# A decoder megakernel on Trainium2: the recurrence's epilogue joined to the routed layer

## The reference, cut to what matters

```
# fifth: a recurrence over 128 steps; of each step only this matters here
y = tanh(g @ L_gy_w.T + L_gy_b + s @ L_sy.T) @ L_yy_w.T + L_yy_b
x = layernorm(x + y)
# sixth: routed layer with sign weights
routing   = softmax(x @ gate_w.T)                    # 8 experts
in_scale  = routing @ in_channel_scale
out_scale = routing @ out_channel_scale
out = (x * in_scale) @ sign(weight).T * out_scale + bias
x = layernorm(x + out)
```

## Time and profile before

| | us |
|---|---|
| median of 3 runs | 3505.43 (3503.76 to 3507.91) |
| the profiled execution's own time | 3504.24 |
| its span in the trace | 3502.4 |

### The profile page before, as it was taken

The page is one execution under the profiler, slowest core; times in us unless marked ns, Lnnn a source line. Parts: engine busy times, 40 slices in busy tenths (PEclk is TensorE's granted clock), DMA queues, the critical chain, the costliest instruction groups (busy, mean ns, idle before and its releaser), DMA issues. The chain is left out here.

```text
span 3502.4 us, 107527 instructions
## 1 busy us (share of the span) xinstructions
PE 3034.8 (87%) x42733; PEld 2061.2 (59%) x42778; DVE 1974.6 (56%) x5167; ACT 1699.7 (49%) x4978; POOL 288.1 (8%) x994
## 2 busy tenths in 40 slices
PE   7876985667999999988989999999999999996898
PEld 4434552336777667754457677676767767762444
DVE  3776776885555555552035555555555555555454
ACT  2333544553444444441136666666666666653433
POOL 1002000000000000001000000000000000002232
PEclk8988997888999999999999999999999999998899
DMA  3002002001000000001123333333333333321100
GB/s 114 8 7 61 11 5 87 0 0 51 1 0 0 0 0 0 0 1 64 35 55 93 88 93 89 91 92 89 93 88 93 88 93 88 93 83 39 49 36 36
DMA packets 287962, 176.19 MB, mean 50 GB/s; under 512 B 23574, under 2 KB 277095, under 8 KB 287901
## 3 DMA queue, kind: packets, MB, share of 16 engines
q1 hardware_dynamic: 284860, 171.16, 16.7%
q0 software_dynamic: 3040, 4.23, 0.6%
HBM read 164.36 MB, written 14.16 MB: 51 GB/s over the span
## 5 line engine op out<-in xcount | busy, mean ns | idle before, releaser
L1987 PE MATMUL ps<-de_hg,st_at 128*32 128x128 f32 x16384 | 516.3, 275 | 0.3 <-DVE st_at L2148 0.3
L1987 PEld LDWEIGHTS ps<-de_hg,st_at 128*32 128x32 f32 x16384 | 424.4, 110 | 31.6 <-DVE st_at L2148 0.5
L2052 ACT ACTIVATE st_th<-ps,st_sw 128x128 f32<-128x128 f32 x1024 | 291.9, 368 | 237.5 <-PE ps L1959 237.5
L2131 DVE TENSOR_TENSOR st_th<-ps,st_sw 128x512 f32<-128x512 f32 x256 | 177.1, 692 | 162.3 <-PE ps L1959 162.3
L1380 PE MATMUL ps<-sa_xt,w_wq 128*128 128x128 f32 x2048 | 239.3, 278 | 0.8 <-ACT sa_xt L1481 0.8
L1380 PEld LDWEIGHTS ps<-sa_xt,w_wq 128*128 128x128 f32 x2048 | 233.5, 194 | 4.9 <-issue 1.4
L1948 PE MATMUL ps<-st_hk,de_cwt 112*32 112x128 f32 x4096 | 164.7, 278 | 79.7 <-DMA st_hk<-padded_alignments 76.1
L1438 PE MATMUL ps<-sa_wo,sa_ct 128*128 128x512 f32 x512 | 222.6, 593 | 0.0
L1499 ACT ACTIVATE sa_pr<-sa_pr,sa_nm 128x128 f32<-128x128 f32 x512 | 197.6, 389 | 7.6 <-DVE sa_nm L1585 7.6
L1959 PE MATMUL ps<-st_fs,de_waf 32*128 32x128 f32 x4096 | 186.5, 296 | 15.8
L2412 PE MATMUL ps<-rf_wb,rf_sp 128*128 128x512 bf16 x737 | 175.3, 385 | 16.9 <-DVEq L2545 15.3
(11 more groups left out here) (400 smaller groups left out, 5816.1 us busy)
## 6 DMA issues: line engine op xcount, KB each, us to landing
st_hk<-padded_alignments SPq DMA_DIRECT2D x254, 448.0 KB, 3.6
X<-in_x_dram SPq DMA_DIRECT2D x16, 512.0 KB, 8.1
out_dram<-X SPq DMA_DIRECT2D x16, 512.0 KB, 2.6
w_wq<-in_Wq_perm_dram SPq DMA_DIRECT2D x1, 4096.0 KB
sa_wo<-in_Wo_perm_dram SPq DMA_DIRECT2D x1, 4096.0 KB, 14.2
gate_inputs<-dp_ro SPq DMA_DIRECT2D x16, 256.0 KB, 2.3
st_rin<-gate_inputs SPq DMA_DIRECT2D x128, 32.0 KB, 3.2
rf_wf<-in_weightT_dram SPq DMA_DIRECT2D x8, 512.0 KB, 6.9
```

The lines of the kernel that those rows point to most:

```text
L1987: ins = pe.matmul(R[g][32 * q:32 * q + 32, :], at[g][:, b, :], hg[:, BG * g + b, q * P:(q + 1) * P], start=False, stop=(b == BG - 1), tile ...
L2052: ins = act.activation(th[g][:, b, :], sums(g, 0)[:, b // 2, (b % 2) * P:(b % 2 + 1) * P], ACT.Tanh, bias=sw[g][:, b:b + 1])
L2131: dve.tensor_tensor(th[g][:, 4:8, :].rearrange("p (k s) n -> p k s n", s=2), sums(g, 1).rearrange("p k (s n) -> p k s n", s=2), sw[g][:, 4 ...
```

## The change

The epilogue stage is gone as a stage of its own. Its code moves into the routed stage, which now gets `sh`, `ah`, `hgy` and the bias rows. The first three batches of y are made and normed at its start; from then on the body of batch b makes and norms batch b+3 (`AHEAD`). The recurrence's large buffers are released earlier by a scope `mid`, the tanh is written over `hgy`, the weights come through four slots instead of eight, and the loading of the last four waits for signs. TensorE's program is written out for all 16 batches; the other engines loop over 12 and have 4 written out.

```diff
 # TensorE, body of batch b
-                def body(b, k, more):
+                pe.wait_ge(y_used, AHEAD)
+
+                for b in range(NB):
+                    k, more = b % 2, b < LAST
                     if more:
                         turn_rows(pe, b + 1, 1 - k)
                     output_scales(pe, b, k)
...
                     if more:
                         input_scales(pe, b + 1, 1 - k)
+                    if b + AHEAD < NB:
+                        make_y(pe, b + AHEAD)
                     layer(pe, b, k, 1)
 # new on TensorE (y_states is the old code of the four groups)
+            def y_bank(b):
+                return 4 if b == 1 else 6
+            def make_y(pe, b):
+                pe.wait_ge(hy_done, b // 4 + 1)
+                if b >= 2:
+                    pe.wait_ge(y_used, b - 1 if b == 2 else b)
+                if b >= AHEAD:
+                    pe.wait_ge(os_kept, b - AHEAD + 1)
+                for h in range(2):
+                    out = ps[:, y_bank(b) + h, :]
+                    pe.matmul(out, hy[:, b, :], lyy[:, h * 512:(h + 1) * 512], start=True, stop=False)
+                    ins = y_bias.add(pe, out, h)
+                ins.then_inc(y_rows, 1)
 # TensorE, ahead of the batches
+                y_states(pe)
+                for b in range(AHEAD):
+                    make_y(pe, b)
+                pe.wait_ge(hy_done, 4)
                 turn_rows(pe, 0, 0)
 # output_scales
                 pe.wait_ge(os_kept, b)
+                pe.wait_ge(y_used, min(b + AHEAD, NB))
 # ScalarE
-                act.preload_act_table(ACT.Exp)
+                act.preload_act_table(ACT.Tanh)
+                eln.start(act)
...
+                eln.apply(act, 0, 0)
+                eln.apply(act, 1, 1)
                 keep_rows(act, 0)
+                signs(range(0, 2))
                 exps(act, 0)
-                for k in range(KH):
...
+                signs(range(2, 4))
+                split(act, 0, 0)
+                eln.apply(act, 2, 0)
+                signs(range(4, KH))
                 keep_rows(act, 1)
                 exps(act, 1)
...
                     ln.apply(act, b, k)
+                    if has(b + AHEAD):
+                        eln.apply(act, b + AHEAD, 1 - k)
 # VectorE
+            def y_row(dve, link, b, k):
+                n = y_bank(b) if isinstance(b, int) else 6
+                dve.wait_ge(y_rows, b + 1)
+                eln.wait_free(dve, b)
+                link(dve.tensor_tensor(eln.row[:, k, :], ps[:, n:n + 2, :].rearrange("p a n -> p (a n)"), tile_of(b), ALU.add))
+                dve.sem_inc(y_used, 1)
...
                 dve.wait_ge(hi_done, b + 1)
                 dve.tensor_tensor(r1[:, :], ys[:, :], sp3[:, k, 0, :], ALU.subtract).then_inc(r_done, 1)
+                if between is not None:
+                    between()                       # y_row of b + 3 in the body of b
                 dve.wait_ge(mid_done, b + 1)
...
+                        if ahead:
+                            eln.statistics(dve, link, 1 - k)
                     r = ln.row[:, k, :]
 # GpSimd, body of batch b
+                    if has(b + 2):
+                        stage_rows(b + 2, k)
+                    if has(b + AHEAD):
+                        eln.factors(pool, link, b + AHEAD, 1 - k)
+                    if has(b + 2):
+                        add_bias(b + 2, k)
+                    ln.factors(pool, link, b, k)
 # SyncE
+                for dst, src in ((lsy, "L_syT"), (gyb, "L_gy_b"), (lyy, "L_yyT")):
+                    sp.dma_start(dst[:, :], a[src]).then_inc(yy_load, 16)
                 sp.wait_ge(cleared, 2)
...
                 for k in range(KH):
+                    if k == 4:
+                        sp.dma_start(bias[:, :], a["bias"].partition_broadcast(P)).then_inc(bias_load, 16)
+                    if k >= 4:
+                        sp.wait_ge(signed, k - 3)
+                    sp.dma_start(wf[:, k % 4, :], a["weightT"][k * P:(k + 1) * P, :]).then_inc(wf_load[k // 2], 16)
```

More of the change, by code:

```diff
@@ L1660, in stage_decoder @@
         y_bias = BiasRows(t)
[L1661 to L1755, removed]
-                            for h in range(2):
[L1757 to L1766, removed]
-                            for k in range(KH):
[L1768 to L1785, removed]
-                        for h in range(2):
-                            act.wait_ge(x_turned, 2 * b + h + 1)
-                            if b >= 2:
-                                act.wait_ge(r_sum, b - 1)
-                            act.copy(xt[:, b % 2, 4 * h:4 * h + 4, :].rearrange("p k n -> p (k n)"), ps[:, 4 + h, :]).then_inc(x_kept, 1)
-                @block.vector
-                def _(dve):
-                    dve.memset(cwt[:, :, :], 0.0).then_inc(blank, 1)
-                    dve.memset(waf[:, :, :], 0.0).then_inc(blank, 1)
-                    dve.wait_ge(w_load, 4 * 16)
-                    for n, (w, _, dst, bias) in enumerate(products()):
-                        dve.wait_ge(summed, n + 1)
-                        if bias is None:
-                            dve.tensor_copy(dst, ps[:, 2 + n % 2, 0:w]).then_inc(summed_kept, 1)
-                        else:
-                            dve.tensor_scalar(dst, ps[:, 2 + n % 2, 0:w], bias, None, ALU.add).then_inc(summed_kept, 1)
-                    dve.wait_ge(halved, 2)
-                    for b in range(NB):
-                        dve.wait_ge(r_sum, b + 1)
-                        if b >= 2:
-                            dve.wait_ge(out[b % 2], 16 * (b // 2))
-                        dve.tensor_tensor(ro[:, b % 2, :], ps[:, 6 + (b + 1) % 2, :], gsb[:, :], ALU.add).then_inc(r_kept, 1)
@@ L2319, in over_tiles, with has @@
                 body(2 * i + 1, 1, True)
-            start(NB // 2 - 1)
-            body(LAST - 1, 0, True)
-            body(LAST, 1, False)
+            start(NB // 2 - 2)
+            for b in range(NB - 4, NB):
+                body(b, b % 2, b < LAST)
+        def has(b):
+            return not isinstance(b, int) or b <= LAST
         with nc.Block() as block:
@@ L2352, in stage_rows @@
                     pool.wait_ge(staged, b + 1)
-                    if isinstance(b, int) and b == 0:
-                        pool.tensor_copy(xs[:, 1, :], tile_of(1)).then_inc(staged, 1)
-                        pool.wait_ge(bias_load, 16)
                     pool.tensor_tensor(xb[:, k, :], xs[:, k, :], bias[:, :], ALU.add).then_inc(biased, 1)
-                ln.start_pool(pool, Chain(pool, pool_seq))
-                stage_rows(0, 0)
-                stage_rows(1, 1)
-                with pool.Fori(0, NB // 2 - 1) as i:
-                    link = Chain(pool, pool_seq, ln.POOL_SETUP + i * 2 * ln.POOL_LINKS)
-                    for k in range(2):
-                        stage_rows(2 * i + k + 2, k)
-                        ln.factors(pool, link, 2 * i + k, k)
@@ L2366, in _ @@
-                link = Chain(pool, pool_seq, ln.POOL_SETUP + (NB - 2) * ln.POOL_LINKS)
-                ln.factors(pool, link, LAST - 1, 0)
-                ln.factors(pool, link, LAST, 1)
+                link = Chain(pool, pool_seq)
+                eln.start_pool(pool, link)
+                ln.start_pool(pool, link)
+                for b in range(2):
+                    eln.factors(pool, link, b, b)
+                for b in range(2):
+                    stage_rows(b, b)
+                eln.factors(pool, link, 2, 0)
@@ new lines, in _, with body @@
+                for b in range(2):
+                    add_bias(b, b)
+                SETUP = 2 * ln.POOL_SETUP + AHEAD * ln.POOL_LINKS
+                def body(b, k, more):
+                    link = state["link"]
+                    if has(b + 2):
[5 more added lines that the diff above has]
+                    ln.factors(pool, link, b, k)
@@ L2370, in turn_rows, with start @@
+                state = {}
+                def start(i):
+                    state["link"] = Chain(pool, pool_seq, SETUP + i * 4 * ln.POOL_LINKS)
+                over_tiles(pool, body, start)
             def turn_rows(pe, b, k):
@@ L2488, in body @@
                         split(act, b + 1, 1 - k)
-                    if not isinstance(b, int) or b < LAST - 1:
+                    if has(b + 2):
                         keep_rows(act, b + 2)
@@ L2507, in softmax_end, with scale_rows @@
                 dve.tensor_copy(rT[:, k, :], RT).then_inc(rT_kept, 1)
[L2509 removed]
+            def y_row(dve, link, b, k):
[4 more added lines that the diff above has]
+                dve.sem_inc(y_used, 1)
+            def scale_rows(dve, link, b, k, between=None):
                 dve.wait_ge(i_sum, b + 1)
@@ L2521, in _ @@
                 dve.memset(rt[:, :, :], 0.0).then_inc(cleared, 1)
+                dve.wait_ge(yy_load, 48)
+                dve.tensor_scalar(lsy[:, :], lsy[:, :], 0.5, None, ALU.mult).then_inc(halved, 1)
                 link = Chain(dve, dve_seq)
+                for b in range(AHEAD):
```

(7 more changed lines are left out.)

894 lines of the change are left out of this document (493 added, 401 removed).

## The result

| | median us | runs | ratio to before, 95% interval |
|---|---|---|---|
| before | 3507.91 | 5 | |
| changed | 3489.46 (3482.80 to 3492.49) | 5 | 0.9944 [0.9927, 0.9961] |
| before, second comparison | 3500.73 | 17 | |
| changed, second comparison | 3477.83 (3475.98 to 3486.04) | 6 | 0.9943 [0.9929, 0.9958] |

What follows compares the result with a forecast made beforehand. Bound: idle stage starts, then the loop's chain of waits through VectorE and ScalarE, with TensorE 93% busy. Terms -48.6 (gap) + 31.4 (loop) + 0.5 (end) = -16.7, giving 3488.8 us by the median; range 3474 to 3506.

Steps and rivals of the forecast that it cites:

- The gap that goes: Between epilogue and routed stages: first product at 3205.7 instead of 3254.28, 48.6 us earlier.
- my walk: Row-by-row reckoning of the joined stage's start with old durations, through exponentials, casts, norm and signs to the first product.
- Table: Start of the joined stage: Exp taken to be in Tanh's preloaded table, cost 0; otherwise one load of 1.28 us.
- The loop: Routed loop with y inside: 2.46 us more a batch than 14.89, through the late copy of `os`; 31.4 in all.
- Batch 0: First batch of the routed loop, at low clock and without the stall: 1.9 us more.
- The written-out program: TensorE's program written out for all batches: cost 0, bounds -1 to +1.28 us a batch.
- The end: One more scope release at the very end of the kernel: 0.5 us.
- Rival 1: In the loop TensorE alone is the bound, no stall for `os`: 1.6 us a batch, 3477.6 in all; chance 0.15.
- Rival 2: In the loop queues cost more than the chain says: up to 3.5 us a batch, 3501.3 in all; chance 0.12.
- Rival 3: In the loop `os` comes so late that the clock falls each batch: 3.0 us more each, 3524.8; chance 0.10.
- Rival 4: TensorE's written-out program stalls in its fetch once a batch, 1.28 us each: 20.5 more, 3509.3; chance 0.08.

Runs made afterwards that it cites:

- the repeated profile: The changed kernel, unedited, run and profiled once more beside the kernel before: batch 17.35 us, ratio 0.9943 of before.
- the combination: Changed kernel with the new norm after the casts, VectorE's new-row statistics in its wait for turned routing, second bias add late at start: 3469.23 us, 0.9920 of before.

## Why the prediction was right

By its steps, from the stage's first instruction, in the first profile:

- *The gap that goes*: 49.1 foretold (48.6, and the 0.5 taken for a release ahead of the stage), 50.8 measured from weight load to weight load, and 49.7 in the repeated profile. By the end of the exponentials it was 2.8 ahead of my walk. Of that, 1.6 is TensorE reaching full clock earlier in the four groups of tanh (first y row after 15.7 and not 17.3 us); it also still had full clock for most of the turned rows (1.26 for 1.97). 1.5 of it went to L2518, where I had no row for a collision because the old start had none. Table: 0, as taken.
- *The loop*: 2.46 a batch foretold, 17.35 measured against 14.88: right to 0.01. Each link is in the rows: the copy of `os` 1.15 later behind the new norm, the wait of 0.77 to 0.86 (0.9), VectorE's statistics done before the row could start (0.67 ahead of L2574, foretold 0.6), the clock at 1.00. The experiments move each: taking the norm or GpSimd's add out shortens the batch, delaying `os` lengthens it. Batch 0 cost 1.8 more than before, foretold 1.9. In all 31.5 for 31.4 (first weight load to the last batch's: 256.6 against 225.2).
- *The written-out program*: 0, shown on the kernel before.
- *The end*: 0.1 for a release taken at 0.5; ahead of the stage 0.4 for 0.5.

Sum -50.8 + 31.5 + 0.1 = -19.2 against my -17.2 for that stretch. The start's 1.7 is the mis-sized term; in the repeated profile it is 0.6, so most of it is the scatter of the start. The mechanism is right. That the forecast of 3488.8 lies 0.7 from the median is luck: single runs lie 10 us apart, the kernel before had its median 2.5 higher than when I forecast, and the second comparison put the gain at 22.9.

Rival 1 (TensorE alone) would have been right only with ScalarE and VectorE both out of its way: 16.49 in the combination, where the rival said 16.5. Rival 2 (up to 3.5 a batch) did not occur: the batch is the chain's 17.35. Rival 3 was priced about right: a stall of 2.9 costs 4.0 a batch in all, where I had 3.0 for one of 2.2. But its condition, a stall of about 2.2 in one piece, does not hold: with y as its bias only the clock fell behind a wait of 1.87 and not behind one of 2.44. Rival 4 did not occur.

What the prediction missed is the collision of VectorE and GpSimd: it took 1.5 us at the start (0.8 in the repeated profile), and the order of the change (add ahead of factors) avoids one in the loop that the seemingly better order runs into.

## What to carry to other kernels

Work moved from an idle stretch into a nearly full loop costs what its longest chain grows by: here 2.46 us a batch for 2.15 on the engine that looked like the bound, since the copy that frees its banks stood behind a new operation of another engine. Walk that chain through the other engines' queues, and walk the second-longest too, for it says how much a repair can bring (0.6 here, of a wait of 0.8). Before swapping two operations of GpSimd, look at which VectorE instruction each will run beside.

## What the runs showed of the hardware

- VectorE's `tensor_scalar` of 128 x 32 fp32, SBUF to SBUF: 0.24 us alone, 2.43 us when started beside GpSimd's `tensor_tensor` of 128 x 1024 (2.36), although VectorE's recorded start is 0.03 to 0.04 earlier. When it starts in the middle of that instruction it ends 0.04 after it (1.04 and 1.72 us).
- Less work on TensorE made its batch no faster in the mean (17.34 against 17.35): the wait ahead of half 0 grew from 0.22 to 1.5 and more, the one ahead of y stayed at 0.8, and the clock fell to 1.2 GHz for a part of four batches. At full clock the batch was 16.7.
- One execution of the changed kernel spent 9 us more than another waiting for a DMA in a stage that the change doesn't touch (86.1 against 76.7 us), half of this change's effect.
